# Summing all weighted states of a two-layer selective scan on TensorE, without folding quads by DMA

## The reference

```python
def step(h, inp):
    dt_t, B_t, C_t, u_t = inp
    dA = jnp.exp(dt_t[:, :, None] * A)
    h = h * dA + (dt_t * u_t)[:, :, None] * B_t[:, None, :]
    y = jnp.einsum('bdn,bn->bd', h, C_t)
    return (h, y)
...
y = jnp.transpose(ys, (1, 0, 2)) + u * D_param
y = y * jax.nn.silu(z)
```

## Time and profile before

| What | Value |
|---|---|
| Runs | 2155.14, 2156.41, 2157.99 us; median 2156.41 us |
| Span of the profiled execution (first to last instruction) | 2153.9 us |
| Time of that execution around its span | not listed; the median run is 2.5 us above the span |
| PE, DVE, ACT, POOL busy | 88%, 90%, 80%, 85% of the span |
| Mean granted clock of PE | 0.968 of full speed |
| First and last scan on DVE start at | 118.6 and 2076.4 us |
| DMA that folds | 64 times 1024 KB, 67.11 MB of 358.77 MB |

### The profile page before, as it was taken

The page is one execution under the profiler, slowest core; times in us unless marked ns, Lnnn a source line. Parts: engine busy times, 40 slices in busy tenths (PEclk is TensorE's granted clock), DMA queues, the critical chain, the costliest instruction groups (busy, mean ns, idle before and its releaser), DMA issues. The chain is left out here.

```text
span 2153.9 us, 22717 instructions
## 1 busy us (share of the span) xinstructions
PE 1887.8 (88%) x5980; PEld 975.5 (45%) x5980; DVE 1935.2 (90%) x2022; ACT 1719.8 (80%) x3125; POOL 1821.9 (85%) x906
## 2 busy tenths in 40 slices
PE   8968789899888989899898989899899988778798
PEld 7533334445354544445454443535445443324356
DVE  5479999999999999999999998999999999899963
ACT  2387788888889888898989888888989987677652
POOL 0088998989898998989899997989989898989950
PEclk9889989999999999999999999999999999899999
DMA  6056665656466575646656675555556666555630
GB/s 247 1 170 174 176 195 150 196 168 185 138 178 176 165 207 166 196 146 180 173 160 187 176 209 155 167 176 164 171 165 195 173 181 179 174 166 176 192 93 20
DMA packets 170543, 358.77 MB, mean 167 GB/s; under 512 B 19544, under 2 KB 27952, under 8 KB 161712
## 3 DMA queue, kind: packets, MB, share of 16 engines
q1 hardware_dynamic: 151958, 279.32, 39.8%
q0 software_dynamic: 9216, 67.11, 15.3%
q10 hardware_dynamic: 9242, 10.89, 1.5%
HBM read 284.85 MB, written 5.29 MB: 135 GB/s over the span
## 5 line engine op out<-in xcount | busy, mean ns | idle before, releaser
L765 POOL TENSOR_TENSOR state<-state,c_rows 128x1024 f32<-128x1024 f32 x512 | 1214.9, 2410 | 139.2 <-DVE state L1328 95.8
L1648 PE MATMUL bank<-state,const_sb 128*128 128x512 f32 x1536 | 775.3, 620 | 111.2 <-POOL state L765 63.7
L1328 DVE TENSOR_TENSOR_SCAN state<-decay,mix_banks 128x512 f32<-128x512 f32 x640 | 753.2, 1207 | 31.5 <-ACT decay L1044 14.5
L1325 DVE TENSOR_TENSOR_SCAN state<-mix_banks,state 128x512 f32<-128x512 f32 x384 | 450.4, 1204 | 30.5 <-ACT mix_banks L1028 19.7
L1648 PEld LDWEIGHTS bank<-state,const_sb 128*128 128x128 f32 x1536 | 282.2, 196 | 423.9 <-issue 252.3
L756 POOL TENSOR_TENSOR state<-kept,b_rows 128x1024 f32<-128x1024 f32 x192 | 469.1, 2443 | 3.4 <-DMA b_rows<-flat_rows 1.7
L1044 ACT ACTIVATE decay<-kept,ssm_pack 128x512 f32<-128x512 f32 x640 | 435.3, 711 | 1.0
L1318 DVE TENSOR_TENSOR mix_banks<-kept,mix_banks 128x1024 f32<-128x1024 f32 x320 | 392.8, 1227 | 28.9 <-ACT mix_banks L1036 19.6
L1028 ACT ACTIVATE mix_banks<-kept,ssm_pack 128x512 f32<-128x512 f32 x384 | 259.5, 683 | 115.7 <-DVE state L1328 101.2
L1544 PE MATMUL bank<-kept,ssm_pack 128*128 128x512 f32 x512 | 244.2, 613 | 25.9 <-DVE kept L1277 8.4
L1036 ACT ACTIVATE mix_banks<-b_rows 128x512 f32<-128x512 f32 x320 | 187.8, 591 | 51.2 <-DVE state L1328 27.6
(11 more groups left out here) (198 smaller groups left out, 2208.7 us busy)
## 6 DMA issues: line engine op xcount, KB each, us to landing
b_rows<-flat_rows SPq DMA_DIRECT2D x512, 256.0 KB, 3.9
c_rows<-flat_rows SPq DMA_DIRECT2D x512, 256.0 KB, 3.6
state<-state POOLq DMA_DIRECT2D x64, 1024.0 KB, 9.7
out<-x_res ACTq DMA_DIRECT2D x8, 512.0 KB, 7.4
ssm_pack<-ssm_pack SPq DMA_DIRECT2D x2, 2035.0 KB, 13.2
x_next<-x ACTq DMA_DIRECT2D x6, 512.0 KB, 7.2
state<-ada_w SPq DMA_DIRECT2D x1, 1536.0 KB, 12.3
kept<-ada_w SPq DMA_DIRECT2D x1, 1536.0 KB, 15.1
```

What stands on the lines that cost most here:

```text
L765: pool.tensor_tensor(st, st, by_pair(c_rows[:, row % ROWS]), ALU.mult).then_inc(m_prod, 1)
L1325: ins = dve.tensor_tensor_scan(st, mixed, st, 0.0, ALU.mult, ALU.add)
L1328: ins = dve.tensor_tensor_scan(st, decay[:, nth(g) % DECAYS], mixed, 0.0, ALU.mult, ALU.add)
L1648: pe.matmul(y_banks[c2][:], ident, state[:, g % STATES], start=False, stop=(g == in_bank[-1])).then_inc(m_sum, 1)
```

## The change

The tuple of folds is empty. Nothing else is edited, but much is derived from it:

```diff
 SUM_LAG = 5
 BANKS, DECAYS, STATES, ROWS = 3, 7, 20, 4
 QUAD = 4
-FOLDS = ((0, 1), (3, 4))
+FOLDS = ()
 FOLD_LAG = 2
 FOLDED_LAG = 14
```

## The result

The median of the changed kernel is 2379.11 us (2375.53 to 2380.02, four runs), that of the kernel before in the same session 2156.95 us (2155.14 to 2157.99, four runs). The ratio is 1.1027, with a 95% interval of 1.1011 to 1.1043: 222 us slower. Forecast were 32, with 86 as the top of the range. The sign was right and the size was not. The profiled execution took 2379.03 us.

A forecast was written before the change was run, and what follows sets the result against it. It took DVE as the bound (95.4% busy in the steady stretch), POOL and PE close behind. Terms 33 + 7 − 6 − 2 gave +32 us on 2156.4, so 2188 us, range 2146 to 2242.

The forecast's parts named there:

- What it moves: First sum and skip of a half go from tick 13 to 5: +7 us of delay, −2 for less crowded last sums.
- The term of PE's work: 256 added matmuls on PE, 220 us, 169 of it in the steady stretch: +33 us, range 0 to +135.
- rival (3): PE becomes the bound outright, streams stay broken and waits stay: +75 to +120, about 2250 us; chance 0.19 with part of rival 4.
- The second reading: Windows with busier PE show 0.29 us of DVE lost per us of PE work: 49 us for 169, a hint only.
- The handshake: At the border of halves, PE's skip must wait for each gate: +7 us counted, between 0 and 43.
- rival 4: Skip and gate make PE and DVE wait for each other: +43 to +96 us; upper half within rival (3)'s 0.19.
- POOL's relief: Without fold issues and transfers POOL gets up to 68 us back: −6 us counted, between 0 and −39.
- rival (1): PE hides all added work, and relief of POOL and the DMA queues decides: faster, 2146 us, at the outside 2117; chance 0.14.
- The last sums: Before the gates and at the kernel's end, sums are less crowded: −2 us, between 0 and −3.4.
- (2): Both effects small: PE costs 5 to 10 us, POOL gives 6 back, 2156 us, no change; chance 0.09.

The follow-up runs named there:

- e14: Changed kernel, whole, with every earlier sum at its old tick and the new sums of quads 0 and 3 14 units behind: 2220.5 us.
- e17: Changed kernel, whole, with the sums of quads 0 to 7 at 12, 10, 10, 12, 10, 8, 6, 6 units behind: 2227.14 us.
- e1: Kernel before, folds kept, with the sums of quads 2 and 5 issued twice, 256 more matmuls on PE: 2235.62 us.
- e18: Changed kernel, whole, with the sums of quads 0 to 7 at 8, 8, 8, 8, 8, 8, 7, 6 units behind: 2277.24 us.
- e9: Kernel before plus bare PE waits for the weighting of quads 0, 1, 3 and 4 five units behind, no matmul moved: 2212.24 us.
- e5: Kernel before with only the two skip matmuls of a half moved to ticks 5 and 6: 2177.02 us.
- e7: Changed kernel, whole, with all sums seven units behind instead of five: 2352.89 us.
- e8: Changed kernel without the sums of quads 0 and 3, all remaining sums, quads 1 and 4 included, five units behind: 2287.39 us.
- e3: Changed kernel without the sums of quads 0 and 3, quads 1 and 4 back at 14 units behind: 2151.16 us.
- e13: e3 plus bare PE waits for the weighting of quads 1 and 4 five units behind, no matmul moved: 2193.47 us.
- e2: Changed kernel with the sums of quads 0 and 3 over 8 columns instead of 512, all waits kept: 2319.08 us.
- e15: Kernel before, folds kept, with quad 2 alone summed nine units behind instead of five: 2239.13 us.
- e16: Kernel before, folds kept, with quad 5 alone summed six units behind instead of five: 2159.75 us.

## Why the prediction was wrong in its size

**What the 222 us are made of.** Three kernels with the same instructions make a ladder. Before to e14: +61, for 220 us more work on PE, on which e17 (+70) and e1 (+77) agree. e14 to e18: +59, for about one sum at every tick, also where PE's other matmuls are bunched. e18 to after: +102, for sums five units behind and a skip at tick 5. For this last step the parts tried alone in the kernel before are the bare waits (54, e9) and the early skip (21, e5); 27 us remain as what they do together, or as error of adding steps that need not add. The run e7 lies between and divides the step otherwise: after to e7, five to seven units behind with the skip still right behind the gates, is only 26 us, though PE's waits for POOL at the sums fall there from 117.5 to 16.5 us. e7 to e18 is the larger part, 77 us, for one unit more of distance (less for the last two quads), the skip at tick 8, mostly clear of the gates, and two ticks of a half without a sum. No run takes these apart. So the early skip may cost more beside even sums than its 21 us alone.

**The failed step** is "What it moves". It priced all that moves at +7 and −2 us. With the same instructions and the same work on PE, after is 159 us slower than e14, so that is what the moves cost. The step's words for the sums are: "The state ring is easier: a sum ran 14 units behind, now 5, with 20 tiles." I took the move of quads 1 and 4 as relief and counted nothing for it. In a kernel with no work added it costs 136 us (e8 against e3), 42 of them the wait alone (e13) and 94 with the new places. For the wait, the 14 units were PE's lead room: at 14 behind, a late PE finds its states ready and works on; at 5 it stops with other engines' matmuls queued behind it. The row that should have warned was in view: in the earlier trace rows POOL's weighting L765 already waits up to 4.4 us for a scan, two ticks and more; five units behind the scan leaves little after that. By the trace of before, a pair's weighting ends 3.0 to 4.9 ticks of 1.93 us after the scan of its first unit starts (mean of 24 halves for each pair; worked out, not a row). The longest are the two pairs of quad 1 (4.9 and 4.2) and the second of quad 0 (4.4), with one each of quads 4 and 5 (4.1): quads 1 and 4 are those that the change moves to 5. The places are the next point.

**The term of PE's work** (+33, between 0 and +135) was mis-sized: 61 to 77 at good places. The step that failed in it was the average: "by pure work PE then needs 1407 of 1500 us, 93.8%: it fits". It fits over 1500 us, not in ticks 4 to 12 of a half, where it is 2.36 of 1.93 us. I had seen that ticks 5 to 12, 17 and 22 to 24 had no sum, and named it in rival (3) as room for catching up; it was the room that the chains used. One half shows it, the seventeenth, cut where DVE starts its scans 4, 13, 26 and 36, before and then after:

```profile
1112.62:1130.29 17.67, 15.55 (x61) 11.49 (x60) 17.42 (x18) 15.26 (x38) 17.45 (x11) 0.90 0.42 128
1130.29:1153.04 22.75, 20.83 (x78) 12.81 (x77) 21.25 (x21) 19.69 (x31) 22.75 (x12) 1.00 0.78 208
1153.04:1171.17 18.13, 14.55 (x41) 6.05 (x40) 16.41 (x14) 18.03 (x52) 16.23 (x10) 1.00 0.59 195
```

```profile
1235.06:1255.59 20.53, 18.46 (x71) 11.95 (x72) 17.53 (x19) 12.65 (x33) 16.89 (x9) 1.00 0.32 115
1255.59:1282.21 26.62, 25.44 (x90) 15.16 (x89) 21.25 (x22) 21.67 (x36) 22.31 (x11) 1.00 0.47 146
1282.21:1300.05 17.84, 11.79 (x26) 4.86 (x25) 16.42 (x15) 17.20 (x49) 15.03 (x10) 0.82 0.38 119
```

In the first part PE goes from 15.55 of 17.67 us to 18.46 of 20.53, and the part is 2.9 us longer. In the second it goes from 20.83 of 22.75 us to 25.44 of 26.62, nearly full, and the part is 3.9 us longer. The third is no longer than before; PE is idle there for 6.05 of 17.84 us, and the mean granted clock of the part is 0.82. So PE is overfull in one part and has time to spare in the next. The 24 middle halves agree (means, worked out from the scans' starts): a half grows by 8.1 us, from 61.8 to 70.0. Of these 4.8 fall in ticks 4 to 12, which go from 20.6 to 25.4 us with PE busy for 24.6 of them, 1.7 in ticks 13 to 20, 1.1 in 21 to 25, 0.6 in 26 to 31 and none in 0 to 3.

**The second reading** of that term, 0.29 us of DVE per us of PE between windows, is near what good places cost (61/220 = 0.28, e14) and tells nothing of bad ones.

**The handshake** (+7, up to 43): +21 alone (e5), within its bounds. That it was the price by itself (rival 4) is excluded by e5; what it adds beside even sums is open (e7 to e18, above). In after DVE's wait at the gate is 11.8 us beside 6.3 in the earlier trace rows, and PE's new wait at the skip is longer than the "under 1 us each" of the forecast, 25.1 us in 8 times:

```profile
PE bank L1638 <- DVE kept L1340: 25.1, 8, 4.5
```

**POOL's relief** (−6, between 0 and −39): −7 by e3. Right, and rival (1)'s first half with it: little is to be had from POOL or the DMA queues.

**The last sums** (−2): not measured apart.

**The rivals.** (1) and (2) fell. (3) had the right engine, and it is the rival nearest to the result, with 0.19. PE wasn't the bound in a steady way, but "streams stay broken" is true, and so is most of "the waits stay": in the 24 middle halves PE is idle 6.0 us a half before and 6.1 after. Its cap of +135 in the stretch took off 34 us for the waits for folds, which other waits replaced, and PE's busy time grew by 8.1 us a half where the added work is 6.9. It named the even spread of the sums, but as lost room for catching up and without a price of its own.

**What the profile should have shown.** Expected were PE at 97% and DVE at 94% of the stretch; after has 91.5% and 84.4%. PE's wait before L1648 was to be shorter; it is somewhat longer than both of its waits of before together (117.5 against 63.7 and 47.0). DVE waits before operations that take a bank as forecast, most at L1217 (52.8), which was named, and L1238 (46.0), which wasn't; L765 and L756 are shorter by 0.05 and 0.08 us:

```profile
L765 POOL TENSOR_TENSOR state<-state,c_rows 128x1024 f32<-128x1024 f32 x512 | 1199.0, 2356 | 406.6 <-DVE state L1328 246.4
...
L756 POOL TENSOR_TENSOR state<-kept,b_rows 128x1024 f32<-128x1024 f32 x192 | 452.8, 2359 | 0.1
```

**Left open.** Why the added work has a floor near 61 us when the count sees room for it (e17), which of the chain matmuls carries the loss at each tick, how far the steps add, what the early skip does beside even sums, and how much of the cost of a place or a wait passes through the clock. No version with all of the work on PE came below before, and only e3, which leaves sums out, did.

## What to carry to other kernels

The distance between a producer and the matmul that takes its result can be lead room of an in-order engine: before shortening it, find which chain matmuls stand behind the wait, and how late the producer can be. Ask of added work whether it fits in each part of the loop, not in its average, and put it where the engine is idle; the same instructions here cost 61 us at good ticks, 120 at a nearly even pace eight units behind, and 222 at an even pace five behind. How much good placing can win must be tried: e17, laid out by the count, was no better than e14. If a change removes a small thing and moves a large one, price the move with a run of its own.

## What the runs showed of the hardware that I had not expected

**Folds slow GpSimd's own operations.** With the folds the weighting and the input on POOL take 2400 and 2436 ns on average in e1 (2410 and 2443 in before), without them 2358 and 2361 in e3 (2356 and 2359 in after). The rows of the weighting in e1, then in e3:

```profile
L766 POOL TENSOR_TENSOR state<-state,c_rows 128x1024 f32<-128x1024 f32 x512 | 1213.6, 2400 | 197.8 <-DVE state L1329 126.7
```

```profile
L768 POOL TENSOR_TENSOR state<-state,c_rows 128x1024 f32<-128x1024 f32 x512 | 1198.3, 2358 | 185.4 <-DVE state L1331 123.0
```

The Trainium skill's page "SBUF — State Buffer" (SBUF: two separate sides) says that a DMA can't be slowed by a compute operation, "and vice versa", and that a DMA issued by GpSimd has its descriptors generated on the GpSimd cores. The 42 ns speak against the first taken alone; the second would explain them. No run here puts the same transfer on another queue, so the cause is only argued.

**Few columns don't make a matmul cheap in proportion.** An instruction of the identity sum over 8 columns lasts 244 ns on average in e2, 620 over 512 columns in after. These are durations, which overlap, not spacings; by spacing, one narrow sum of two instructions starts at 1073.13 us in e2 and the next matmul at 1073.27, so it takes 0.14 us, a sixth of the 0.86 of a full one for a 64th of the columns. The rows of e2:

```profile
L1650 PE MATMUL bank<-state,const_sb 128*128 128x8 f32 x512 | 81.9, 244 | 55.2 <-POOL state L766 55.2
```

```profile
1073.13 0.28 PE L1650 MATMUL bank<-state,const_sb 128*128 128x8 f32 x2
1073.27 1.10 PE L1639 MATMUL bank<-kept,skip_diag 128*128 128x512 f32 x2
```

**The clock adds to a late PE.** Mean granted clock over the execution is 0.954 in after, 0.968 in before and 0.974 in e14, where PE is busy 93% of the span. With two levels, 0.5 and 1 of full speed, that is 9% of after's span at the lower one against 6% of before's, some 80 us more; as work takes twice its time there, it can explain at most 40 of the 222.

In the runs that add no work or less of it, the same bound is larger, and this is a rival that no run excludes. The clock is 0.929 in e8 against 0.958 in e3, at most 72 of the 136 us between them; 0.945 in e9 and 0.938 in e15, against about 0.964 in the kernel before beside them, at most 44 of 54 and 61 of 80; and 0.926 in e2, which may hide up to 62 us of what the full width costs. On the other side, a lower clock alone need not cost time: e3 at 0.958 is faster than before, and the profiled run of e16, at 0.955, is within 5 us of its median. In the windows of 1184 to 1195 us above, the clock fell around a wait of 3.54 us, so it may be part of how a wait or a bad place costs time, but the 136 and 54 us can't be taken over into the 222 as they stand.
